# First attention of a two-layer block: row maxima over 1024 columns in two double banks, bursts of four scores, whole value products

## The reference

```python
qkv = jnp.einsum('bsc,oc->bso', x, w_qkv).reshape(B, S, 3, H, D)   # H = 16 heads, D = 16
q = layer_norm(qkv[:, :, 0], q_gamma, q_beta)
k = layer_norm(qkv[:, :, 1], k_gamma, k_beta)
q, k = apply_rope(q, k)
attn = jnp.einsum('bqhd,bkhd->bhqk', q * scale, k)
attn = jax.nn.softmax(attn, axis=-1)                               # 1024 keys, no mask
out = jnp.einsum('bhqk,bkhd->bqhd', attn, v).reshape(B, S, C)
```

## Time and profile before

| | |
|---|---|
| time, median of 3 runs | 1919.41 us (1919.35 to 1925.64) |
| profiled execution, first to last instruction | 1920.6 us |
| mean granted clock of TensorE | 0.956 |
| TensorE busy | 1801.7 us (94%) |
| VectorE busy | 1429.7 us (74%) |
| ScalarE busy | 1116.8 us (58%) |
| maxima of the first attention, 1024 reductions | 621.3 us |
| exponentials of the first attention, 1000 in the score banks | 523.9 us |

### The profile page before, as it was taken

How to read it: one execution, slowest core, us unless ns; L and a number is a source line. 1 busy time by engine, 2 the same in 40 slices (tenths; PEclk the granted TensorE clock), 3 DMA queues, 4 the chain that set the end, 5 groups by cost and what they waited for, 6 DMA issues and landing times. The chain is left out here.

```text
span 1920.6 us, 34540 instructions
## 1 busy us (share of the span) xinstructions
PE 1801.7 (94%) x12658; PEld 1172.6 (61%) x12658; DVE 1429.7 (74%) x2814; ACT 1116.8 (58%) x2212; POOL 531.4 (28%) x686
## 2 busy tenths in 40 slices
PE   8989999999999999799999979999999986999995
PEld 4545444444444444488888855556555565999994
DVE  7879999999999999266677655566666544766665
ACT  4645888888888888623232214455364632655555
POOL 5750000333000001142223112212525243444444
PEclk9976999999999999899999978998999998999997
DMA  4883744564334502123354255545566334655555
GB/s 168 286 251 52 123 84 90 135 147 116 82 57 81 85 18 82 34 61 110 110 169 160 88 191 125 144 100 134 154 152 155 89 98 141 154 156 146 142 113 197
DMA packets 146598, 239.16 MB, mean 125 GB/s; under 512 B 25829, under 2 KB 81158, under 8 KB 146448
## 3 DMA queue, kind: packets, MB, share of 16 engines
q1 hardware_dynamic: 113312, 171.48, 36.4%
q0 software_dynamic: 17024, 34.25, 6.8%
q10 hardware_dynamic: 16112, 31.46, 4.6%
HBM read 137.49 MB, written 96.60 MB: 122 GB/s over the span
## 5 line engine op out<-in xcount | busy, mean ns | idle before, releaser
L994 DVE TENSOR_REDUCE b_mx<-b_PM 128x1 f32<-128x512 f32 x1024 | 621.3, 679 | 19.4 <-PE b_PM L848 19.0
L970 ACT ACTIVATE b_probs<-b_PS 128x512 f32<-128x512 f32 x1000 | 523.9, 606 | 70.4 <-PE b_PS L902 55.1
L848 PE MATMUL b_PM<-b_kst,b_qst 48*128 48x512 f32 x888 | 281.4, 431 | 0.0
L2912 ACT ACTIVATE d_probs<-d_PS 128x512 f32<-128x512 f32 (+3 forms) x384 | 166.4, 496 | 191.4 <-PE d_PS L2815 190.8
L902 PE MATMUL b_PS<-b_qst,b_kst 50*128 50x512 f32 x744 | 256.8, 436 | 3.2 <-issue 1.2
L2951 DVE TENSOR_REDUCE d_mx<-d_PM 128x2 f32<-128x1024 f32 (+1 forms) x192 | 179.8, 950 | 102.4 <-PE d_PM L2767 57.4
L902 PEld LDWEIGHTS b_PS<-b_qst,b_kst 50*128 50x128 f32 x744 | 120.5, 184 | 164.2 <-ACT b_probs L970 147.4
L2867 POOL TENSOR_SCALAR_AFFINE_SELECT d_probs<-d_probs 128x128 f32<-128x128 f32 x256 | 75.2, 307 | 273.9 <-ACT d_probs L2912 269.2
L790 POOL CAST b_mhalves<-b_maxima 128x16 fp32r<-128x16 f32 x32 | 6.3, 197 | 505.6 <-DVE b_maxima L1003 505.6
L848 PEld LDWEIGHTS b_PM<-b_kst,b_qst 48*128 48x128 f32 x888 | 142.1, 185 | 5.2
L874 PE MATMUL b_PO<-b_probs,x_v 128*32 128x384 f32 (+2 forms) x2048 | 145.2, 390 | 0.0
(11 more groups left out here) (316 smaller groups left out, 3739.0 us busy)
## 6 DMA issues: line engine op xcount, KB each, us to landing
halves<-a_parts SPq DMA_DIRECT2D x7, 2048.0 KB, 8.7
qk<-c_halves ACTq DMA_DIRECT2D x7, 2048.0 KB
w_w<-L_ffn_fc1T SPq DMA_DIRECT2D x12, 1024.0 KB, 5.0
w_w<-L_ffn_fc2T SPq DMA_DIRECT2D x12, 1024.0 KB, 6.3
b_qst<-halves SPq DMA_DIRECT2D x72, 128.0 KB, 4.4
b_kst<-halves SPq DMA_DIRECT2D x72, 128.0 KB, 7.5
d_qst<-qk SPq DMA_DIRECT2D x36, 256.0 KB, 5.0
d_kst<-qk SPq DMA_DIRECT2D x36, 256.0 KB, 7.0
```

Of the source, the lines that this page charges most:

```text
L848: mm = pe.matmul(PM[n % MBANKS][:], qst[buf][at, p, first:first + P], kst[buf][at, p, kh * BLK:(kh + 1) * BLK], start=True, stop=True)
L970: act.activation(probs[:, s % RING], score_bank(g, s)[:], ACT.Exp).then_inc(exped, 1)
L994: dve.tensor_reduce(mx[:, half, (r * PAIRS0 + p) * TPH + t, kh:kh + 1], PM[n % MBANKS][:], AX.X, ALU.max)\
L2912: act.activation(probs[:, s % RING, 0:w], PS[bank(s)][:, 0:w], ACT.Exp).then_inc(exped, 1)
```

## The change

The row maximum of a step is taken over all 1024 keys by one reduction. `PM` becomes two tiles of two banks each; the first product of a step waits for the tile, the second tells VectorE. The joining reduction and its semaphore go. A burst is a whole round, four scores with the four products of two maximum steps, then, where the turn is due, the turn, then the value products of the round before, whole. The plan in quarters, its break and the repeated products go. The number of score banks stays at three. The turn moves to units 24 and 56, the copy of `PO` to the end of the first round of the next half. In the last group the wide stretch begins at unit 24.

```diff
-    TURN_UNITS = [23, 55]
+    TURN_UNITS = [24, 56]
-    SBANKS, MBANKS = 3, 4
+    SBANKS, MTILES = 3, 2
...
-    LAG, BREAK = 6, 3
-    REPEATS = {7: 3, 8: 2, 9: 2, 10: 2}
-
-    def quarters_through(k):
...
-    def values_after(k):
...
-        PM = [a.ps(f"PM{i}", [P, BLK]) for i in range(MBANKS)]
+        PM = [a.ps(f"PM{i}", [P, HALVES, BLK]) for i in range(MTILES)]
...
-            def max_product(g, x, kh, times=1):
+            def max_product(g, x, kh):
                 half, t, p, r = step_at(x)
-                n, buf, first = (g * STEPS + x) * HALVES + kh, g % BUFS, half * BLK + t * P
+                n, buf, first = g * STEPS + x, g % BUFS, half * BLK + t * P
                 at = slice(r * ROWS0, r * ROWS0 + K)
-                pe.wait_ge(max_taken, n + 1)
-                for _ in range(times):
-                    mm = pe.matmul(PM[n % MBANKS][:], qst[buf][at, p, first:first + P],
-                                   kst[buf][at, p, kh * BLK:(kh + 1) * BLK], start=True, stop=True)
-                mm.then_inc(max_scores, 1)
+                if kh == 0:
+                    pe.wait_ge(max_taken, n + 1)
+                mm = pe.matmul(PM[n % MTILES][:, kh], qst[buf][at, p, first:first + P],
+                               kst[buf][at, p, kh * BLK:(kh + 1) * BLK], start=True, stop=True)
+                if kh == HALVES - 1:
+                    mm.then_inc(max_scores, 1)
...
-            def values(g, R, first, end):
+            def values(g, R):
                 half, kt = R // TPB, R % TPB
-                cols = slice(first * BLK // G0, end * BLK // G0)
-                if first == 0:
-                    pe.wait_ge(exped, g * UNITS + (R + 1) * G0 + SBANKS)
-                    if kt == 0:
-                        pe.wait_ge(out_copied, g * HALVES + half + 1)
+                pe.wait_ge(exped, g * UNITS + (R + 1) * G0 + SBANKS)
+                if kt == 0:
+                    pe.wait_ge(out_copied, g * HALVES + half + 1)
                 for i in range(G0):
                     j = head_of(g, R * G0 + i)
-                    mm = pe.matmul(PO[j * VS0:(j + 1) * VS0, cols], ...
+                    mm = pe.matmul(PO[j * VS0:(j + 1) * VS0, :], ...
...
-            def burst(g, k):
-                for s in units_of(k):
+            def burst(g, R):
+                for s in range(R * G0, (R + 1) * G0):
                     score(g, s)
-                for i, at in enumerate(TURN_PLACES):
+                for i, first in enumerate(TURN_UNITS):
                     u = HALVES * g + 1 + i
-                    if at // SBANKS == k and u < TURNS:
+                    if first == (R + 1) * G0 and u < TURNS:
-                        pe.wait_ge(exped, g * UNITS + exps_before(at - SBANKS + 1) + SBANKS)
+                        pe.wait_ge(exped, g * UNITS + exps_before(TURN_PLACES[i] - SBANKS + 1) + SBANKS)
                         turn_max(u)
-                for before, R, first, end in values_after(k):
-                    if g + before >= 0:
-                        values(g + before, R, first, end)
+                if R > 0:
+                    values(g, R - 1)
+                elif g > 0:
+                    values(g - 1, ROUNDS - 1)
...
-                    if s == COPY_UNITS[1] and g > 0:
+                    if s == G0 - 1 and g > 0:
                         copy_out(g - 1, 1)
-                    if s == COPY_UNITS[0]:
+                    if s == UNITS // HALVES + G0 - 1:
                         copy_out(g, 0)
...
-                dve.tensor_reduce(mx[:, half, (r * PAIRS0 + p) * TPH + t, kh:kh + 1], PM[n % MBANKS][:], AX.X, ALU.max)\
-                   .then_inc(max_taken, 1)
-
-            def join_maxima(u):
...
+                dve.tensor_reduce(maxima[:, half, r * PAIRS0 + p, t:t + 1], PM[n % MTILES][:].rearrange("p h n -> p (h n)"),
+                                  AX.X, ALU.max).then_inc(max_taken, 1)
```

More of the change, by code:

```diff
@@ L597, in phase_attention0 @@
     LAPS = UNITS + len(TURN_UNITS)
[L598 to L605, removed]
+    assert LAPS % SBANKS == 0 and HALF_STEPS % MTILES == 0 and UNITS % RING == 0
+    assert len({at % SBANKS for at in TURN_PLACES}) == 1 and all(first % G0 == 0 for first in TURN_UNITS)
     WIDE_FROM = TURN_UNITS[0]
-    WIDE_BURST = place(WIDE_FROM) // SBANKS
-    WBANKS = MBANKS + SBANKS
-    assert place(WIDE_FROM) % SBANKS == 0 and bank(WIDE_FROM - 1) == 1
+    WBANKS = MTILES * HALVES + SBANKS
     def wide(g, s):
@@ L681, in phase_attention0 @@
         PT = PS[TURN_PLACES[0] % SBANKS][:, 0:P]
-        WIDE = [*PM, PS[bank(WIDE_FROM - 2)], PS[bank(WIDE_FROM - 1)], PS[TURN_PLACES[0] % SBANKS]]
+        WIDE = [*(tile[:, kh] for tile in PM for kh in range(HALVES)),
+                *(PS[b][:] for b in (bank(WIDE_FROM - 2), bank(WIDE_FROM - 1), TURN_PLACES[0] % SBANKS))]
         def score_bank(g, s):
-            return WIDE[(s - WIDE_FROM) % WBANKS] if wide(g, s) else PS[bank(s)]
+            return WIDE[(s - WIDE_FROM) % WBANKS] if wide(g, s) else PS[bank(s)][:]
         setup, ones_made, ones_set = a.sem("setup"), a.sem("ones_made"), a.sem("ones_set")
-        max_scores, max_taken, max_made = a.sem("max_scores"), a.sem("max_taken"), a.sem("max_made")
+        max_scores, max_taken = a.sem("max_scores"), a.sem("max_taken")
         m_high, m_cut, m_turned, m_copied, rows_in = (
@@ L861, in turn_max @@
                 pe.transpose(PT, mhalves[:].rearrange("p n r i m -> p (n r i m)"), ident).then_inc(m_turned, 1)
-            def values(g, R, first, end):
+            def values(g, R):
                 half, kt = R // TPB, R % TPB
-                cols = slice(first * BLK // G0, end * BLK // G0)
-                if first == 0:
-                    pe.wait_ge(exped, g * UNITS + (R + 1) * G0 + SBANKS)
-                    if kt == 0:
-                        pe.wait_ge(out_copied, g * HALVES + half + 1)
+                pe.wait_ge(exped, g * UNITS + (R + 1) * G0 + SBANKS)
+                if kt == 0:
+                    pe.wait_ge(out_copied, g * HALVES + half + 1)
                 for i in range(G0):
                     j = head_of(g, R * G0 + i)
[L874 to L877, removed]
+                    mm = pe.matmul(PO[j * VS0:(j + 1) * VS0, :], vst[g % BUFS][:, kt, j, :], probs[:, (R * G0 + i) % RING],
+                                   start=(kt == 0), stop=(kt == TPB - 1), tile_position=(0, j * VS0))
+                mm.then_inc(pv_done, 1)
             def score(g, s):
@@ L888, in score @@
                 if wide(g, s):
[L889 to L890 removed]
+                    if w < MTILES * HALVES:
+                        pe.wait_ge(max_taken, MTILES + TURNS * HALF_STEPS)
                     elif w == WBANKS - 1:
@@ L932, in _ @@
             for g in range(GROUPS):
-                for k in range(BURSTS if g < GROUPS - 1 else WIDE_BURST):
-                    burst(g, k)
-            s, v = WIDE_FROM, quarters_through(WIDE_BURST - 1)
+                for R in range(ROUNDS if g < GROUPS - 1 else WIDE_FROM // G0):
+                    burst(g, R)
+            s = WIDE_FROM
             for R in range(WIDE_FROM // G0 + 1, ROUNDS + 2):
@@ L939, in _ @@
                     s += 1
-                values(GROUPS - 1, R - 2, v % G0, G0)
-                v += G0 - v % G0
-            assert v == UNITS
+                values(GROUPS - 1, R - 2)
         @block.scalar
@@ L985, in _ @@
         def _(dve):
-            dve.sem_inc(max_taken, MBANKS)
+            dve.sem_inc(max_taken, MTILES)
             def take(n):
-                x, kh = n // HALVES % STEPS, n % HALVES
-                half, t, p, r = step_at(x)
+                half, t, p, r = step_at(n % STEPS)
+                if n % HALF_STEPS == 0 and n // HALF_STEPS >= HALVES:
+                    dve.wait_ge(m_cut, n // HALF_STEPS - 1)
                 dve.wait_ge(max_scores, n + 1)
-                dve.tensor_reduce(mx[:, half, (r * PAIRS0 + p) * TPH + t, kh:kh + 1], PM[n % MBANKS][:], AX.X, ALU.max)\
-                   .then_inc(max_taken, 1)
-            def join_maxima(u):
[L999 to L1006, removed]
+                dve.tensor_reduce(maxima[:, half, r * PAIRS0 + p, t:t + 1], PM[n % MTILES][:].rearrange("p h n -> p (h n)"),
+                                  AX.X, ALU.max).then_inc(max_taken, 1)
+            for n in range(TURNS * HALF_STEPS):
                 take(n)
-                if n % HALF_MAXIMA == 0 and n > 0:
-                    join_maxima(n // HALF_MAXIMA - 1)
-                if n == HALVES * (TOTALS_GROUP - 1) * HALF_MAXIMA:
+                if n == (TOTALS_GROUP - 1) * STEPS:
                     dve.wait_ge(totals_in, 16)
                     dve.reciprocal(first_totals[:], first_totals[:]).then_inc(shares_made, 1)
-            join_maxima(TURNS - 1)
             dve.wait_ge(totals_in, 32)
```

10 lines of the change are left out of this document (4 added, 6 removed).

## The result

The changed kernel takes 1969.77 us (median of 4 runs, 1966.82 to 1976.27) beside 1919.38 for the kernel before: the ratio is 1.0271, 95% interval 1.0252 to 1.0290. 1965 was forecast, in a range of 1938 to 1988.

The account below looks back on a forecast made before the run. TensorE with ScalarE bounds the kernel before; afterwards three score banks for four scores do. Half 21.26 for 19.70 us: 29 halves +45.2, last group +1.3, opening -1.0, together +45.5, so 1965 us, range 1938 to 1988.

Parts of the forecast that it names:

- the chain of TensorE with ScalarE: First attention, kernel before: these two engines set the half of 19.70 us; VectorE, needing 19.3, follows just behind.
- The ring: Bursts of four, three score banks: fourth score waits for its burst's first exponential; round 1.18 + 0.43 + 0.99 = 2.60 us.
- Turn and copy: Once a half: the maxima's transpose waits for one more exponential, 0.36 us; the values' copy delays an exponential by 0.10.
- The opening: 16 maximum steps before the first score: VectorE is ready sooner with 1024-column maxima, -1.0 us once.
- The cover of 0.6 us: Double maximum banks: the product needing a tile comes early enough before the next score is due, so they cost nothing.
- The repeats: Five extra maximum products a half are removed; they ran beside scores that waited anyway, so no effect on time.
- The rival of the clock: TensorE's idle 0.2 us a round lowers the clock in a fifth of the 29 halves: 2047 us, chance 0.06.
- The two effects cancel: Rival for the first attention: round 2.45 us, half 19.8, about 1921 us in all; chance 0.05.

Follow-up runs that it names:

- The last run: The kernel before without the break in the value products at the start of a half and without the repeated maximum products; 1909.3 us, ratio 0.9946.
- The 384-column run: The changed kernel with value products of 384 columns instead of 512 in seven of the eight rounds of a half; 1932.9 us, ratio 1.0071.
- the run with whole steps: The changed kernel with value products between third and fourth score, both products of a burst's second maximum step behind the fourth score; 1968.6 us, ratio 1.0270.
- the run in halves: The changed kernel with value products in two pieces of 256 columns, behind the second and the fourth score; 1944.2 us, ratio 1.0122.

## Why the prediction was right

**What bounds the kernel.** The prediction put the half of before down to the chain of TensorE with ScalarE, VectorE just behind. The last run bears that out: with the break gone the half falls by 0.2 to VectorE's own rate and stops there. So VectorE stood 0.2 us a half behind the chain, not the 0.4 of the prediction's sum. In bursts of four, single and double maxima give the same half to an exponential: there a cheaper VectorE pays nothing, as forecast.

**The ring.** Its terms came out as 1.18, 0.44 and 0.99 for 1.18, 0.43 and 0.99. The 384-column run shows that the value products lie in it one for one, the run with whole steps that it doesn't hang on where the burst is cut, the run in halves that it goes when two scores stand between value products.

**Turn and copy.** The half is 21.28 less 8 x 2.61 = 20.88, so 0.40 for both, with 0.46 forecast. At the turn, the fourth score, transpose and value products begin as follows:

```profile
459.81 0.50 PE L856 MATMUL b_PS<-b_qst,b_kst 50*128 50x512 f32 x1
...
460.30 0.33 PE L818 MATMUL b_PS<-const,b_mhalves 128*128 128x128 f32 x1
460.55 1.06 PE L829 MATMUL b_PO<-b_probs,b_vst 128*32 128x512 f32 x8
```

0.74 from score to value products instead of 0.44: 0.30, just under the 0.32 that the prediction had as its lowest.

**The opening, mis-sized.** -1.0 was forecast for the maxima before the first score, and 0 for the first half. In the profiled run the first exponential comes 2 us later than before and the second half begins 6 us later. VectorE's timeline in the opening, the kernel before first:

```profile
137.81 14.43 DVE L994 TENSOR_REDUCE b_mx<-b_PM 128x1 f32<-128x512 f32 x24
```

```profile
140.60 2.36 DVE L947 TENSOR_REDUCE b_maxima<-b_PM 128x1 f32<-128x1024 f32 x2 [0.18 <-PE b_PM L804]
143.14 2.36 DVE L947 TENSOR_REDUCE b_maxima<-b_PM 128x1 f32<-128x1024 f32 x2 [0.17 <-PE b_PM L804]
```

Two steps take 2.54 us, 1.27 each, where two single maxima took 2 x 0.598 = 1.20, here too ((14.43 - 0.68)/23 = 0.598). The clock is 0.50 in both. Every second step VectorE now waits 0.17 to 0.18 us for a product, a wait that the term of -1.0 had left out; 16 steps make 1.2 of the 2 us. The step that failed is this term: it took VectorE's rate at full clock, with a tile always ready. All runs with double banks have the first exponential at 162.8 to 163.2, those with single banks at 160.8 to 161.2.

The other 4 us go with the clock, which rose at 182.9 us (the window from 180 to 185 has 0.71) instead of about 174, the time that the prediction had kept. In the profiles with single banks it rose between 171.4 and 177.2, in those with double banks between 169.8 and 199.5, later than 177 in four of six. With one profile of each, what decides it stays open.

**Double banks, repeats and break.** The cover of 0.6 us for the double banks was there: at full clock TensorE's products wait for them 0.5 us in all, its weight loads 2.6. The repeats were put at nothing because they ran beside waiting scores. In the changed kernel, which has no break, no cost of leaving them out shows: its clock stays at 1.00. But the reason was not the whole of it: in the kernel before they hold the clock, and removing them alone costs 0.46%.

**The rival of the clock.** It did not happen: 1.00 from 190 to 807, though TensorE stands idle 617.00 - 590.14 = 26.9 us in 232 rounds, 0.12 us a round for the 0.2 given. The Trainium skill, "TensorE: Matmul & The Clock Gate", section A second HAM failure mode: psum-queue depth-cycling, warns of short idle times between groups of products; the changed kernel's rows don't show it; in the kernel before without repeats the clock did fall to 0.50, behind gaps in its breaks.

**A rival's sum.** "The two effects cancel" is added up wrong: a round of 2.45 with the turn's 0.32 and the copy's 0.10 is a half of 20.0 and about 1929 us, not 19.8 and 1921. It did not happen either way.

**The sum.** 29 halves +45.8 by 21.28 - 19.70 (45.2 forecast); the profiled span grew by 1974.4 - 1920.6 = 53.8. Of the other 8.0 the start of the second half has 6.0, and the last group and what follows it about 2, with 1.3 forecast. The medians differ by 50.4, for 45.5 forecast: the ring's term was right, the opening's and the clock's were not.

## What to carry to other kernels

Before a burst is made longer, count the banks that it fills, from one long piece of TensorE's work (here the value products) to the next: n products over fewer than n banks wait for the engine that empties them, and everything behind them in TensorE's order takes that wait each time. A tile that is filled by two products belongs wholly to one burst; split by long work in between, it stalls both engines, as the double banks did in bursts of three. And an engine that nobody waits for gives nothing back when it gets faster: look who waits for VectorE before VectorE's work is cut.

## What the runs showed that was not expected

The same double banks cost 79 us in bursts of three (2000.1 - 1920.9, both from one chip) and nothing in bursts of four. "Perfetto Trace Analysis" in the Trainium skill, section Optimizing Scalar/DVE Operations, says that where VectorE isn't saturated but leaves gaps on other engines, smaller instructions may finish the work sooner; in bursts of three the trace agrees, 83.8 us of VectorE idle and 47.6 us of weight loads waiting for a reduction, against 5.6 and none. No run separates the larger instruction from the split of a step over two bursts.

Five extra products a half, made beside scores that wait, hold the clock at 1.00 in the kernel before. Without them it went to 0.50 in some of the breaks, mostly for 3.4 us, in the case shown from a stretch in which TensorE was still busy 1.86 of 2.30 us; in the wide stretch of the kernel before, 4.02 of 5.00 busy had kept 1.00.
